# Turning normalised tiles in the ternary passes: TensorE transposes replaced by VectorE's 32x32 blocks and a trip through DRAM

## The reference, cut to what matters

```python
x = x + 0.5 * _L0_ffn_ref(_layernorm(x), W1, W2, W3)         # passes 0, 1 (kind A)
x = x + _L0_attn_ref(_layernorm(x), qkv, o_proj, gamma, beta) # attention
x = x + 0.5 * _L0_ffn_ref(_layernorm(x), W1, W2, W3)         # passes 2, 3 (kind A)
x = x + 0.5 * _L1_ffn_ref(_layernorm(x), gate_w, up_w, down_w, ...)   # passes 4, 5 (kind B, ternary)
x = x + _L1_attn_ref(_layernorm(x), B, C, D)                  # state space, with the skip D * x
x = x + 0.5 * _L1_ffn_ref(_layernorm(x), gate_w, up_w, down_w, ...)   # passes 6, 7 (kind B, ternary)
```

## Time and profile before

| | |
|---|---|
| time, median of 3 runs | 1694.33 us (1693.45 to 1696.97) |
| time of the profiled execution | 1695.64 us |
| its span in the trace | 1693.8 us |
| PE busy | 1684.5 us, 99% of the span |
| PE's weight loads | 1392.2 us, 82% |
| DVE busy | 1169.8 us, 69% |
| ACT busy | 820.1 us, 48% |
| POOL busy | 125.7 us, 7% |
| TensorE clock granted | 0.999 of full speed |
| DRAM traffic | 357.13 MB, 211 GB/s on average |

### The profile page before, as it was taken

The page is one execution under the profiler, slowest core; times in us unless marked ns, Lnnn a source line. Parts: engine busy times, 40 slices in busy tenths (PEclk is TensorE's granted clock), DMA queues, the critical chain, the costliest instruction groups (busy, mean ns, idle before and its releaser), DMA issues.

```text
span 1693.8 us, 21648 instructions
## 1 busy us (share of the span) xinstructions
PE 1684.5 (99%) x7611; PEld 1392.2 (82%) x7611; DVE 1169.8 (69%) x1832; ACT 820.1 (48%) x1335; POOL 125.7 (7%) x185
## 2 busy tenths in 40 slices
PE   9999999999999999999999999999999999999998
PEld 7788888888888888888888888888888788888887
DVE  8888778667776554755446655447668869877866
ACT  5745444465575543433223333223556456655644
POOL 1000000000012220000000000000000143100001
PEclk9999999999999999999999999999999999999999
DMA  9778866699985000257544457444666663366765
GB/s 321 266 307 297 286 261 229 240 367 365 368 337 205 1 1 1 82 170 235 177 163 176 160 172 233 148 162 146 251 228 202 254 224 113 127 242 231 251 224 212
DMA packets 129596, 357.13 MB, mean 211 GB/s; under 512 B 36304, under 2 KB 57680, under 8 KB 124112
## 3 DMA queue, kind: packets, MB, share of 16 engines
q1 hardware_dynamic: 129488, 355.73, 58.4%
HBM read 268.12 MB, written 87.56 MB: 210 GB/s over the span
## 4 chain that ended last, share of the span: by engine, by line
PE 92%; DVE 3%; DMA 2%; SPq 1%; issue 1%; ACT 0%; ACTq 0%; DVEq 0%
PE psum L597 34%; PE psum L599 30%; PE psum L601 26%; PE psum L917 2%; DMA x<-in_w2a 1%; DMA mix_kept<-mix_prep 1%; SPq L744 1%; DVE xc_lo L2139 0%; DMA flat<-in_w3a 0%; DMA w<-w_kept 0%; DMA mix_in_raw<-mix_raw 0%; DVE att_lo L2108 0%; PE psum L1194 0%; DVE fw_lo L2102 0%; SPq L700 0%
## 5 line engine op out<-in xcount | busy, mean ns | idle before, releaser
L597 PE MATMUL psum<-xc_hi,w 128*128 128x512 f32 x1544 | 603.6, 391 | 1.8 <-DMA w<-w_kept 1.0
L599 PE MATMUL psum<-xc_lo,w 128*128 128x512 f32 x1544 | 601.0, 389 | 0.0
L601 PE MATMUL psum<-xc_hi,w 128*128 128x512 f32 x928 | 361.1, 389 | 0.0
L597 PEld LDWEIGHTS psum<-xc_hi,w 128*128 128x128 f32 x1544 | 289.8, 188 | 66.5 <-DVE psum L2218 1.8
L599 PEld LDWEIGHTS psum<-xc_lo,w 128*128 128x128 f32 x1544 | 289.9, 188 | 59.3
L597 PE MATMUL psum<-w,hid 128*128 128x512 f32 x864 | 337.6, 391 | 0.0
L601 PE MATMUL psum<-w,hid 128*128 128x512 f32 x864 | 336.4, 389 | 0.0
L2181 DVE TENSOR_TENSOR x<-psum,x 128x512 f32<-128x512 f32 x256 | 173.1, 688 | 147.1 <-PE psum L601 146.6
L599 PE MATMUL psum<-w,hid 128*128 128x512 f32 x544 | 211.7, 389 | 0.0
L601 PEld LDWEIGHTS psum<-xc_hi,w 128*128 128x128 f32 x928 | 174.2, 188 | 36.4
L1550 ACT ACTIVATE psum<-psum 128x512 f32<-128x512 f32 x108 | 62.8, 582 | 285.9 <-PE psum L601 219.6
(11 more groups left out here) (178 smaller groups left out, 2010.9 us busy)
## 6 DMA issues: line engine op xcount, KB each, us to landing
w<-w_kept SPq DMA_DIRECT2D x93, 896.0 KB, 6.9
w<-w_kept SPq DMA_DIRECT2D x130, 512.0 KB, 7.2
w<-w_kept SPq DMA_DIRECT2D x57, 640.0 KB, 4.3
w_kept<-w SPq DMA_DIRECT2D x16, 1792.0 KB, 7.6
w<-w_kept SPq DMA_DIRECT2D x93, 256.0 KB, 4.3
w_kept<-prep SPq DMA_DIRECT2D x12, 1792.0 KB, 7.6
w_kept<-w SPq DMA_DIRECT2D x16, 512.0 KB, 7.0
turn_scratch<-swap SPq DMA_DIRECT2D x48, 128.0 KB, 2.5
```

The source lines that it names most:

```text
L597: pe.matmul(out, a_hi, b_hi, start=start, stop=False, skip_group_check=onto)
L599: last = pe.matmul(out, a_hi, b_lo, start=False, stop=stop and zero == "a", skip_group_check=onto)
L601: last = pe.matmul(out, a_lo, b_hi, start=False, stop=stop, skip_group_check=onto)
```

## The change

Passes 4, 5 and 6 join `SWAPPED`. Their 24 tiles are turned by VectorE (`swap_pair` in `ternary_slot`, between the last result of a down product and `sum_c22`), and TensorE's transposes and ScalarE's `turn_out` in these passes are gone. The trip through DRAM has a new form in all six passes: `swap` and the scratch are laid out so that a pair of tiles is stored by one transfer of 128x4 pieces of 1 KB, and a chunk (two pairs) is loaded by four transfers, each of 32x32 pieces of 256 bytes. In a ternary pass the store stands between the first part of the weights and the wait for p4, and the load at the end of SP's work for a slot. POOL's skip waits for the swap and not for the transposes. In pass 6 the norms move to slots 4 to 7, and `sums` of pass 7 from slots 8 and 9 to slots 9 and 10.

```diff
-FIRST_SUMS, LAST_SUMS = {8: 0, 9: 2}, {8: 1, 9: 3}
+FIRST_SUMS = {5: {8: (0,), 9: (2,)}, 7: {9: (0,)}}
+LAST_SUMS = {5: {8: (1,), 9: (3,)}, 7: {9: (1, 2), 10: (3,)}}
-NORMS = {4: (3, 4, 5, 6), 5: (4, 5, 6, 7), 6: (4, 4, 5, 6), 7: ()}
-SWAPPED = (0, 2, 3)
+NORMS = {4: (3, 4, 5, 6), 5: (4, 5, 6, 7), 6: (4, 5, 6, 7), 7: ()}
+SWAPPED = (0, 2, 3, 4, 5, 6)
-TURNS = {4: (4, 5, 6, 7), 5: (5, 6, 7, 8), 6: (4, 5, 6, 7), 7: ()}
...
-    turn_scratch = nc.dram_tensor("turn_scratch", [BLOCK, P // BLOCK, KD, P // BLOCK, 2 * BLOCK], F32).ap()
+    turn_scratch = nc.dram_tensor("turn_scratch", [2, KD, 2 * P // BLOCK, BLOCK, P // BLOCK, 2 * BLOCK], F32).ap()
-        swap = at("swap", [P, P // BLOCK, KD, BLOCK, 2], F32, "xn", 4 * KIB)
+        swap = at("swap", [P, KD, P // BLOCK, BLOCK, 2], F32, "xn", 4 * KIB)
...
+            def turn_store(ps, k):
+                sp.wait_ge(swapped, swaps_before(ps) + 2 * k + 2)
...
+                rows = slice(k % 2 * P // BLOCK, (k % 2 + 1) * P // BLOCK)
+                sp.dma_start(turn_scratch[k // 2][:, rows, :, :, :].rearrange("k a i b t -> (a i) k (b t)"),
+                             swap[:, :, :, :, :].rearrange("p k b j i -> p k (b j i)")).then_inc(turn_stored[ps.no], 16)
+            def turn_load(ps, c):
+                sp.wait_ge(turn_stored[ps.no], 32 * (c + 1))
+                if ps.kind == "B" and c == 0:
+                    sp.wait_ge(c22_read, ps.u0 + 3)
+                if ps.kind == "B" and c:
+                    sp.wait_ge(down_ready, ps.downs[4][-1][2] + 1)
                 for b in range(P // BLOCK):
...
+                    sp.dma_start(xs[b * BLOCK:(b + 1) * BLOCK, 2 * c:2 * c + 2, :, :].rearrange(
+                                     "p h k (a t) -> p (h k a) t", t=2 * BLOCK),
+                                 turn_scratch[c][:, :, :, b, :].rearrange("k a i t -> i (k a) t")).then_inc(turn_in[ps.no], 16)
...
-                    else:
-                        bank_free("n", n)
-                        pe.wait_ge(xn_ready, plan.norm_base[ps.no] + tile + 1)
-                        turn(xn[:, tile % 4, :], plan.bank["n", n]).then_inc(turn_ready, 1)
...
-                pool.wait_ge(turn_ready, n + 1)
-                skip(xn[:, tile % TT, :], x[:, tile, :], xn[:, tile % TT, :])
+                pool.wait_ge(swapped, swaps_before(passes[BEFORE_S - 1]) + tile + 1)
+                skip(xn[:, tile % 2, :], x[:, tile, :], xn[:, tile % 2, :])
...
+                if s in ps.norms:
+                    swap_pair(ps, ps.norms.index(s))
                 sum_c22(u)
                 gated(ps, s)
```

More of the change, by code:

```diff
@@ L136, in add_pass @@
         self.passes.append(ps)
-        if no not in (BEFORE_T - 1, len(PASSES) - 1):
+        if no in SWAPPED:
             self.norm_base[no] = self.norm
@@ L165, in add_pass @@
                         ps.turns[s].append((n, n))
[L166 to L170, removed]
         if kind == "B":
@@ L470, in paired @@
         def paired(no):
-            return no - 1 in SWAPPED
+            return no not in (0, BEFORE_T, BEFORE_S)
         def of_unit(u):
@@ L627, in w13_load @@
                     w13_part(v, block, FIRST_W, w13_in)
+                if between:
+                    turn_store(*between)
                 if low_before:
@@ L831, in _ @@
                                  ps.u0 + s - 1 if ps.kind == "B" and s else None, not early,
-                                 ps.kind == "B" and s - 1 in AHEAD)
+                                 ps.kind == "B" and s - 1 in AHEAD,
+                                 (ps, ps.norms.index(s - 1)) if ps.kind == "B" and s - 1 in ps.norms else None)
                     else:
@@ L1682, in ternary_slot @@
                         norm_pair(ps, k)
-                for n, tile in ps.turns[s]:
-                    turn_out(n, tile, plan.bank["n", n])
                 if s == ps.n - 2:
@@ L2006, in _ @@
             pool.wait_ge(skip_in, 16)
-            for n, tile in (tt for tiles in passes[BEFORE_S - 1].turns for tt in tiles):
+            for tile in range(PT):
                 if tile == 2:
                     chunk()
-                pool.wait_ge(turn_ready, n + 1)
-                skip(xn[:, tile % TT, :], x[:, tile, :], xn[:, tile % TT, :])
+                pool.wait_ge(swapped, swaps_before(passes[BEFORE_S - 1]) + tile + 1)
+                skip(xn[:, tile % 2, :], x[:, tile, :], xn[:, tile % 2, :])
             chunk()
@@ L2424, in ternary_slot @@
                     return
-                if follower(ps) and s in FIRST_SUMS:
-                    sums(follower(ps), FIRST_SUMS[s])
+                if follower(ps):
+                    for step in FIRST_SUMS[ps.no + 1].get(s, ()):
+                        sums(follower(ps), step)
                 behind = bool(ps.downs[s]) and s not in ps.open
@@ L2439, in ternary_slot @@
                     extra(ps, s, k + 1)
-                if follower(ps) and s in LAST_SUMS:
-                    sums(follower(ps), LAST_SUMS[s])
+                if follower(ps):
+                    for step in LAST_SUMS[ps.no + 1].get(s, ()):
+                        sums(follower(ps), step)
+                if s in ps.norms:
+                    swap_pair(ps, ps.norms.index(s))
                 sum_c22(u)
@@ L2478, in state_low @@
             def state_low(c, j):
-                low(("s", c, j), hid[:, 2 * (c % 2) + j, :, :], sg[:, j, :], BEFORE_S)
+                low(("s", c, j), hid[:, 2 * (c % 2) + j, :, :], sg[:, j, :], "S" if c < 2 else BEFORE_S)
             def state_x_low(c, i):
```

81 lines of the change are left out of this document (33 added, 48 removed).

## The result

| | median, us | runs |
|---|---|---|
| before | 1695.58 | 9 (1693.45 to 1698.64) |
| changed | 1701.14 | 9 (1695.10 to 1706.80) |

The changed kernel is slower: the ratio of the runs is 1.0034, with a 95% interval of 1.0023 to 1.0044. I had forecast 1687.3 us, 7.0 us or 0.4% faster, and given slower 5%. Its runs also spread over 12 us where those of before spread over 5. The profiled execution is its quickest, 1695.10 us; a later one of the same kernel is shown with e11.

A forecast was written before the change was run, and what follows sets the result against it. PE was taken to bound the kernel, busy 1684.5 of 1693.8 us. 10.4 saved, less 3.0 in pass 5 and 0.4 in pass 6, made 7.0 us off 1694.33: 1687.3 us, range 1683.4 to 1691.4.

The forecast's parts named there:

- What PE loses, 10.4 us: Passes 4 to 6: 12 groups of eight transposes leave PE at 0.87 us each, 10.4 us less.
- Eight pairs hidden in passes 4 and 6: Block transposes of 1.29 us a pair fit DVE's idle time there, 0.28 us left, so they cost nothing.
- Rival D: The pair is late in all 12 slots, eight more at 0.5 us: 1691.3 us; chance 0.15.
- The waits of PE in the earlier trace: Over the kernel's whole span, PE's longest wait is 1.0 us, for weights at the start of pass 5.
- Pass 6, slot 9, 0.4 us: A third `sums` of 1.22 us ahead of a `sum_c22` with no idle costs 0.4 us.
- Pass 5, 3.0 us: DVE's full slots 4 and 5, and POOL's skip beside DVE in slots 4 to 7, make PE wait 3.0 us.
- the density: Pass 5, slots 4 and 5: DVE is too full to hide the pair; 1.4 of the 3.0 us.
- The form in passes 0, 2 and 3, 0 us: The trip's new form costs nothing there: same bytes, 15 us slots, DMA 71% busy.
- The trip in the ternary passes, 0 us: DMA is asked 11.7 us per 10.0 us slot, but the lead covers the backlog: 0, bounds 0 and +12 us.
- Rival C: Slower than before through the 256-byte loads, by SP's issue time or slow pieces: about 1718 us, mild form 1699; chance 0.06.
- C's mild form: DMA bound at 11.0 us a slot in the trips' 12 slots, 12 us more: 1699 us; within the 0.06.
- The 256-byte pieces: Trip's loads: by the rule for pieces under 512 bytes, as slow as the old 256-byte stores, the sum unchanged.

The follow-up runs named there:

- e11: The changed kernel itself timed and profiled once more, beside the other runs on the same chip: 1702.16 us, 1.0039 of before.
- e6: Changed kernel with a branch on SP that skips loading the low halves of w1 and w3 in passes 4 to 7 where weights are exact: 1690.23 us.
- e9: Kernel before, with the same SP branch, so no low halves of the ternary weights are loaded in passes 4 to 7: 1695.88 us, 0.9997.
- e7: e6 with POOL's skip in pass 5 left out (an addition of 8 columns a tile in its place): 1685.74 us, 0.9935.
- e4: Kernel before, with the new form of the trip in passes 0, 2 and 3 alone; passes 4 to 6 keep their transposes on TensorE: 1696.05 us, 0.9999.
- e1: Changed kernel, but in passes 4 to 6 a chunk's four loads bring the same 1 MB in 1 KB instead of 256-byte pieces: 1700.85 us, 1.0022.
- e2: Changed kernel, but the load of the low halves of w1 and w3 in passes 4 to 7 brings a fourteenth of its columns: 1689.49 us, 0.9956.
- e8: e6, but pass 5 keeps its 32 transposes on TensorE, with POOL's skip behind them as before: 1689.03 us, 0.9956.
- e12: Changed kernel, with half of the columns of the low halves of w1 and w3 loaded in passes 4 to 7: 1692.35 us, 0.9979.
- e3: Changed kernel, but the first sums of pass 5 stands at the head of slot 9 of pass 4, not slot 8: 1698.96 us, 1.0014.

## Why the prediction was wrong, point by point

- **What PE loses, 10.4 us: right.** e6 against e9 is 3.6 us in pass 4 and 3.4 in pass 6, where the sum had 3.5 each; e7 against e9 is 9.6 us by the stages and 1695.88 - 1685.74 = 10.1 us by the medians.
- **Eight pairs hidden in passes 4 and 6: right.** 0.36 us of idle time is left in front of `gated_first`, and e6 has no wait of PE for DVE there. Rival D falls.
- **The waits of PE in the earlier trace rows: misread, without effect.** The longest of the kernel before is 1.3 us, for POOL's `warm` at 1.33 us from the start, and not 1.0; nothing rests on it.
- **Pass 6, slot 9, 0.4 us:** small as forecast: 3.4 where 3.5 less 0.4 was due.
- **Pass 5, 3.0 us: the sum nearly right, its parts not.** e6 against e7 is 3.4 us by the stages, 4.5 by the medians. It is the skip, with both `hid_low` of every slot doubled and more, and next to nothing is the density. I had priced one instruction made longer by 0.77 us; the two `hid_low` of a slot grow by 1.97 us together, each beside one POOL instruction. The places were wrong as well: of PE's three waits one is in slot 4 (0.59 us) and two are in slot 5 (0.69 and 1.21), where `gated_second` is slowed too (1.34 us instead of 0.75); slots 6 and 7, to which I gave 0.5 each, show none of over 0.2. That the sum came out near 3.0 is luck in good part.
- **The form in passes 0, 2 and 3, 0 us: right** (e4).
- **The trip in the ternary passes, 0 us: this step failed.** The prediction put the trip at nothing because the backlog has a lead. By e11 against e6 it costs 5.0 us in pass 4, 3.3 in pass 5 and 3.7 in pass 6, 12 us, the upper bound that I had given; by the medians it is 11.9. The quick execution pays 1.5, 1.3 and 5.0, so the share of each pass is that of an execution. The demand was estimated well: a pair's trip asks for 4.5 us of all 16 engines by the packets (4096 pieces of 24.0 ns for a chunk's loads, 512 of 46 ns for each store) where I had 4.2. Wrong was the sentence "weights are asked for a slot and more ahead; a backlog of 4 x 1.7 = 7 us at worst has about 10 us of lead". The weights have that lead, nearly: in e11 PE waits 0.9 us for them in passes 4 to 6. The trip has not, and it goes through the same queue: the last store lands behind the weights (5.6 us instead of 3), the loads may start only then, and take ten more; between the last swap of the pass and `sums` lie some 15 us, and both legs have to fit in. The third store has the first chunk's loads in front of it besides, and the last pair's transposes wait for it. I asked whom the backlog delays among those who were there before, and not whether it delays the newcomer. A length of the trip could have been read from the kernel before: in pass 3, from the first store at 1007.17 to the last landing of the loads, 2.7 us after their issue at 1012.92, it takes 8.5 us with the engines 0.71 busy.
- **Rival C was the right side with the wrong reason.** SP's issue of a load took 1.4 to 2.6 us on average of four, and single ones 3.5 to 8.1, not 0.9, so the forecast was wrong on that as well and C's condition (one of the four over 2 us) was met in every chunk of passes 4 to 6. But e1 takes this away and gains nothing. By size, C's mild form, "DMA bound", 1699 us, came near; it had every slot of the trips longer, and what happened is a landing behind `sums` and one behind a swap, in single slots. I gave C 6% in all, on the ground of the lead.
- **The 256-byte pieces decided little either way.** In the ternary passes a chunk's loads ask for 6.1 us of all engines as 4096 pieces of 256 bytes and for about 5.2 (an estimate from the packets below: 1024 of 81 ns) as 1 KB pieces in e1, and no time comes back.
- Without that step the forecast stands: e6, with the trip on time, measured 1690.23 beside a before of 1696.71, 6.5 us less, or 5.7 less than e9, where 7.0 was forecast.
- **Not tried.** That the trip waits behind the weights is shown by e2, e6 and the order of the landings; whether it would be quicker issued from another engine, or with the store ahead of the weights that SP issues for the slot after next, no run shows, nor whether the order comes from SP's one queue or from engines that are full.

The best kernels here that compute the reference for any weights are e8 and e6, 0.44% and 0.39% under before. Each needs both edits: the swaps alone lose, the lighter weights alone do nothing.

## What to carry to other kernels

When work moves from the bounding engine to a round trip through DMA, the first thing to price is the latency of the new trip behind the traffic that is already there, from its last producer to its first consumer, and not only whether the old traffic can bear more. A transfer that nobody waits for in the kernel before can be the one to remove after the change: its bytes were free and are not any more. And a two-input POOL operation that is moved next to DVE's two-input ones should be priced by every pair of instructions that can meet, not by one.

## What the runs showed of the hardware

- The same four loads of 1024 pieces held SP from 5.46 to 10.55 us in one kernel; as 256 pieces each they held it for 1.80 to 3.59 us and landed no sooner (e1). In pass 3, with less traffic, four such loads held SP for 3.1 us (from 1009.62) in the changed kernel. Issue time and landing time are different things here.
- Pieces of 1 KB that go to 32 partitions were slow in e1's packet records: 1464 packets of 1 KB, 1024 of them such loads, took 71 ns on average from 1231.1 to 1242.9 us, where the 512 of the store before took 46. With 46 ns for the other 440 that makes about 81 ns for a piece of the loads (an estimate). 256-byte pieces took 24.0 ns in the changed kernel: a quarter of the pieces took over three times as long each.
- A store that was issued while the transfer before it was still under way landed 1.2 to 1.4 us behind that one in eight of eleven cases in the changed kernel, whether this made 3.0 or 6.4 us from its issue; the other three landed 1.9 to 2.8 us behind.
- A wait of PE of 2.38 us (pass 6, quick execution) or 2.58 us (e11) was followed by some three microseconds at the lower clock, worth about 1.6 us. The length of the wait alone doesn't tell: waits of 1.94 and 1.87 us in e12 were followed by eight matmuls 0.43 us apart, one of 2.64 us in e3 (1556.52) by none. After waits of 0.5 to 1.5 us in the changed kernel the matmuls started 0.23 us apart again after one of 0.34.
- A branch on SP over a value in SBUF, ahead of four passes' loads, cost nothing that can be seen (e9, 0.9997).
